# A two-layer graph network on one core: projecting with the sums as the stationary operand, 14 node slots per tile, and a new table of tiles looked up by TensorE

## The reference, cut to what matters

```python
h = relu(layernorm(x))
# layer 0: a row of 9 edge coefficients times the source's 32 features, contracted with W
x = x + segment_sum(einsum over (coef9[e], h[src[e]], W), dst)
h = relu(layernorm(x))
# layer 1: 16 basis coefficients by relation, times an attention scalar, and the last edge's self loop
a   = tanh(relu(sum(x_hat * y_hat) / sqrt(32)))      # x_hat from h[src], y_hat from h[dst], relation
msg = einsum("eb,ebo->eo", w_comp[etype], einsum("ei,bio->ebo", h[src], weight))
x = x + relu(segment_sum(a * msg, dst) + h[src[last edge]] @ self_loop_weight)
```

## Time and profile before

| what | value |
| --- | --- |
| median of the runs | 3294.89 us |
| time of the profiled execution | 3295.84 us |
| its span in the trace | 3294.0 us |
| PE busy | 2972.4 us, 90% |
| PEld busy | 2392.0 us, 73% |
| DVE busy | 2602.5 us, 79% |
| POOL busy | 2414.9 us, 73% |
| ACT busy | 895.1 us, 27% |
| POOL's gathers, L541 | 2541, mean 946 ns |
| found rows, L609 | 8190 matmuls, mean 372 ns |

### The profile page before, as it was taken

The page is one execution under the profiler, slowest core; times in us unless marked ns, Lnnn a source line. Parts: engine busy times, 40 slices in busy tenths (PEclk is TensorE's granted clock), DMA queues, the critical chain, the costliest instruction groups (busy, mean ns, idle before and its releaser), DMA issues.

```text
span 3294.0 us, 108331 instructions
## 1 busy us (share of the span) xinstructions
PE 2972.4 (90%) x41934; PEld 2392.0 (73%) x41934; DVE 2602.5 (79%) x3897; ACT 895.1 (27%) x1910; POOL 2414.9 (73%) x2546
## 2 busy tenths in 40 slices
PE   2999999999999999999789999999999999899997
PEld 2777777777777777777677777777777777777776
DVE  7777777777777777777678888888888888888886
ACT  1111111111111111111344444444444444444342
POOL 6777777777777777777377777777777777777774
PEclk9999999999999999999789999999999999999998
DMA  4111111111111111111233333333333333332331
GB/s 138 28 28 28 28 28 28 27 28 27 28 27 29 27 29 27 29 27 29 67 55 58 55 59 59 57 56 59 58 57 56 59 58 58 55 58 54 58 57 40
DMA packets 220288, 150.94 MB, mean 46 GB/s; under 512 B 122954, under 2 KB 201083, under 8 KB 219901
## 3 DMA queue, kind: packets, MB, share of 16 engines
q0 software_dynamic: 81312, 41.79, 12.3%
q1 hardware_dynamic: 138013, 100.79, 12.3%
q10 hardware_dynamic: 576, 2.40, 0.2%
HBM read 136.54 MB, written 8.22 MB: 44 GB/s over the span
## 4 chain that ended last, share of the span: by engine, by line
PE 32%; POOL 9%; issue 5%; DVE 4%; DVEq 1%; DMA 0%; ACT 0%; POOLq 0%; ACTq 0%
PE ps L609 17%; POOL xg L541 9%; PE ps L634 5%; PE ps L675 4%; PE ps L622 3%; DVE scratch L960 2%; PE ps L657 1%; PE ps L572 1%; PE ps L645 1%; DVE Z L1044 0%; DMA xg<-h_table,idx 0%; DVE aggT L1062 0%; DVEq L960 0%; DVE blocks L951 0%; DVEq L1062 0%
## 5 line engine op out<-in xcount | busy, mean ns | idle before, releaser
L541 POOL DMA_INDIRECT xg<-h_table,idx x2541 | 2404.1, 946 | 844.1 <-issue 758.9
L609 PE MATMUL ps<-h,blocks 128*128 128x448 f32 x8190 | 1803.0, 372 | 237.5 <-DVE scratch L960 213.4
L609 PEld LDWEIGHTS ps<-h,blocks 128*128 128x128 f32 x8190 | 1501.3, 188 | 458.5 <-issue 324.1
L1044 DVE TENSOR_TENSOR Z<-coef,ps 128x864 f32<-128x864 f32 (+1 forms) x522 | 734.4, 1448 | 16.6 <-DVE ps L985 0.2
L951 DVE TENSOR_TENSOR blocks<-scratch,ps 128x896 fp32r<-128x896 int16 x585 | 630.1, 1077 | 34.4 <-PE ps L609 34.4
L675 PE MATMUL ps<-Z,xg 128*32 128x32 f32 (+3 forms) x25008 | 507.8, 215 | 8.3 <-DVE Z L1044 7.9
L675 PEld LDWEIGHTS ps<-Z,xg 128*32 128x32 f32 x25008 | 403.9, 110 | 93.0 <-issue 70.2
L1062 DVE TENSOR_TENSOR aggT<-aggT,ps 64x128 f32 (+1 forms) x262 | 74.1, 283 | 485.1 <-PE ps L657 478.4
L960 DVE SCALAR_TENSOR_TENSOR scratch<-ramp_sb,scratch,ps 128x448 f32<-128x448 f32 x585 | 396.7, 678 | 7.8
L830 ACT ACTIVATE p_left<-ps 96x128 f32<-96x128 f32 (+2 forms) x262 | 64.6, 246 | 1189.3 <-PE ps L645 1140.8
L965 DVE TENSOR_REDUCE xg<-scratch 128x32 f32<-128x448 f32 x585 | 362.8, 620 | 20.2
(11 more groups left out here) (105 smaller groups left out, 1109.4 us busy)
## 6 DMA issues: line engine op xcount, KB each, us to landing
xg<-h_table,idx POOLq DMA_INDIRECT x2541
rows_b<-typ_short SPq DMA_DIRECT2D x130, 258.0 KB
scratch<-q_short SPq DMA_DIRECT2D x260, 96.0 KB
rows_b<-dst_short SPq DMA_DIRECT2D x130, 126.0 KB
coef<-in_edge_dram SPq DMA_DIRECT2D x130, 54.0 KB
att_tab<-p_table SPq DMA_DIRECT2D x393, 8.1 KB
p_table<-Z SPq DMA_DIRECT2D x8, 297.0 KB, 3.9
X<-in_x_dram SPq DMA_DIRECT2D x7, 224.0 KB, 4.6
```

The lines of the kernel that those rows point to most:

```text
L541: pool.indirect_dma_start(xg[:, g.q, t - g.s * J, :], None, h_table[n], bass.IndirectOffsetOnAxis(ap=idx[:, t:t + 1], axis=0)).then_inc(L. ...
L609: last = pe.matmul(found_ps[b], blocks[:, b, c, :], h_2[:, a, c], start=(c == 0 and a == 0), stop=(c == NCH - 1 and a == 1))
L1044: dve.tensor_tensor(Z[:, b, js, 0:C * WN].rearrange("p j (c n) -> p j c n", n=WN), coef[:, js, :].unsqueeze(3).broadcast_to([P, k, C, WN]) ...
```

## The change

- WN is 14 in place of 16. HW, the width of a half group, becomes 84 in place of 96. `Z` and the startup tables share a buffer `room` of fixed size.
- `project` has the sums stationary (84 columns) and the weights moving (64 or 32 columns), one chain over c for each half: 6 matmuls in place of 3 in layer 0, 10 in place of 5 in layer 1. Its result has nodes on partitions. `copy_oT`, `turn` and their buffers are gone.
- `place_rows` of g-2 comes after tile 4 of the 12 in `sum_edges`, where `turn` was, in place of after tile 8.
- `copy_o` comes ahead of the attention in ScalarE's step.
- `NP` has an entry for each group. Layer 0: 2 in the first 8 and last 8 groups, else 3, 3, 3, 2 in turn, 346 found tiles in place of 325. Layer 1: 3 in every fourth group from 8 to 116, else 2, 288 in place of 260.
- ScalarE, VectorE and SyncE have 16 steps straight, 11 rounds of a loop of eight steps, and the rest straight. The flag `beyond` is read at step 16 on each engine, in place of after the steps.
- TensorE waits for the last `added` itself; VectorE's wait and signal for it are gone.

```diff
-WN = 16
+WN = 14
 JH = J // 2
 HW = JH * WN
 NCH = 7
 MC = M // NCH
-NP = [[3, 2, 3, 2], [2, 2, 2, 2]]
+EIGHT = 8
+LOOP = [2, FULL // EIGHT - 3]
+NP = [[2 if s < 8 or s >= FULL - 8 else [3, 3, 3, 2][s % 4] for s in range(FULL)], [3 if 8 <= s < FULL - 10 and s % 4 == 0 else 2 for s in range(FULL)]]
 NPM = max(max(np) for np in NP)
...
-    return len(range(q, FULL, 4)) * (J - NP[n][q]) + (JT if q == FULL % 4 else 0)
+    return sum(J - np for np in NP[n][q::4]) + (JT if q == FULL % 4 else 0)
+
+
+def in_loop(count, i, r):
+
+    if isinstance(i, int):
+        return count(i * EIGHT + r)
+    at = LOOP[0] * EIGHT + r
+    return count(at) + (i - LOOP[0]) * (count(at + EIGHT) - count(at))
 
 
...
             return gathers_of_pass(n, self.q)
-        return (self.i + self.r // 4 + 1) * (J - NP[n][self.q])
...
 
-        return self.nj if self.tail else J - NP[n][self.q]
+        return self.nj if self.tail else J - NP[n][self.of_loop()]
...
         if self.tail:
             return []
-        np = NP[n][self.q]
-        return [(NPM - np + i, J - np + i, (sum(NP[n][0:self.q]) + i) % 2, self.tiles_before(n) + i + 1) for i in range(np)]
+        at = self.of_loop()
+        np = NP[n][at]
+        return [(NPM - np + i, J - np + i, (sum(NP[n][0:at]) + i) % 2, self.tiles_before(n) + i + 1) for i in range(np)]
 
 
...
-def over_steps(eng, k, body, lag):
+def over_steps(eng, k, body, lag, look):
 
 
     def step(i, r):
-        body([Group(i, r - d, k) if not isinstance(i, int) or 0 <= i * 4 + r - d < NG else None for d in range(lag + 1)])
-    for t in range(4):
+
+        body([Group(i, r - d, k) if not isinstance(i, int) or 0 <= i * EIGHT + r - d < NG else None for d in range(lag + 1)])
+    for t in range(LOOP[0] * EIGHT):
         step(0, t)
-    with eng.Fori(0, FULL // 4 - 1) as i:
-        for u in range(4):
-            step(i, 4 + u)
-    for t in range(FULL // 4 * 4, NG + lag):
+    too_far = look(eng) if isinstance(k, int) else None
+    with eng.Fori(*LOOP) as i:
+        for u in range(EIGHT):
+            step(i, u)
+    for t in range(LOOP[1] * EIGHT, NG + lag):
         step(0, t)
-
-
-def all_steps(body, lag):
+    return too_far
+
+
+def all_steps(eng, body, lag, look):
 
     for s in range(NG + lag):
+        if s == LOOP[0] * EIGHT:
+            too_far = look(eng)
         body([Group(0, s - d, 0) if 0 <= s - d < NG else None for d in range(lag + 1)])
+    return too_far
 
...
-        oT_ps = ps[0:2 * F, 4, :]
-        o_ps = ps[0:HW, 4, 2 * HW:2 * HW + 4 * F].rearrange("p (h o) -> p h o", h=2)
-        win_ps = ps[0:3 * F, 4, 2 * HW + 4 * F:2 * HW + 4 * F + P]
+        o_ps = ps[0:HW, 4, 0:4 * F].rearrange("p (h o) -> p h o", h=2)
+        win_ps = ps[0:3 * F, 4, 4 * F:4 * F + P]
...
-        Z = sb("Z", [P, 2, J, C1 * WN])
-
-
-        room = Z[:].rearrange("p b j z -> p (b j z)").bitcast(I32)
+        room = sb("room", [P, max(2 * J * C1 * WN, 4 * T)], I32)
+        Z = room[:].bitcast(F32)[:, 0:2 * J * C1 * WN].rearrange("p (b j z) -> p b j z", b=2, j=J)
         dst_all, dnext_all, first_all, group_all = (room[:, i * T:(i + 1) * T] for i in range(4))
...
+        def look_beyond(eng):
+
+            eng.wait_ge(beyond_set, 1)
+            return eng.value_load(beyond[0:1, 0:1], min_val=0, max_val=1)
+
         def all_passes(eng, passes, restart=None, finish=None):
 
-            passes(0)
-            eng.wait_ge(beyond_set, 1)
-            too_far = eng.value_load(beyond[0:1, 0:1], min_val=0, max_val=1)
+            too_far = passes(0)
             with eng.If(too_far):
                 if restart:
...
                     for s in range(NG):
+                        if s == LOOP[0] * EIGHT and isinstance(k, int):
+                            too_far = look_beyond(pool)
                         gather(Group(0, s, k))
+                    return too_far
 
                 all_passes(pool, one_pass)
...
                     pe.wait_ge(L.G_set, g.order())
-                    wait(pe, L.oT_set, g.order() - 1)
+                    wait(pe, L.o_set, g.order() - 1)
                     wait(pe, L.added, g.order() - 1)
-                    for c in range(cq):
-                        rows = P if c < cq - 1 else F
-                        last = pe.matmul(oT_ps[0:no, 0:hh * w], weights[0:rows, c, :], G_sb[0:rows, c, 0:hh, 0:w],
-                                         start=(c == 0), stop=(c == cq - 1))
+                    for h in range(hh):
+                        for c in range(cq):
+                            rows = P if c < cq - 1 else F
+                            last = pe.matmul(o_ps[0:w, h, 0:no], G_sb[0:rows, c, h, 0:w], weights[0:rows, c, :],
+                                             start=(c == 0), stop=(c == cq - 1))
                     last.then_inc(L.projected, 1)
-
-                def turn(g):
-                    hh, w = g.halves()
-
-                    pe.wait_ge(L.oT_set, g.order())
-                    wait(pe, L.o_set, g.order() - 1)
-                    pe.nop().then_inc(L.turn_go, 1)
-                    for h in range(hh):
-                        last = pe.transpose(o_ps[0:w, h, 0:no], oT_sb[0:no, h, 0:w], ident[0:no, 0:no])
-                    last.then_inc(L.turned, 1)
 
                 def place_rows(g):
...
@@ -678,8 +685,6 @@
                         if j == g.nj - 1:
                             last.then_inc(L.summed, 1)
                         if back and j == min(g.nj, J // 3) - 1:
-                            turn(back)
-                        if back and j == min(g.nj, 2 * J // 3) - 1:
                             place_rows(back)
 
                 def step(gs):
@@ -693,18 +698,16 @@
                     if gs[1]:
                         sum_edges(gs[1], gs[2])
                     elif gs[2]:
-                        turn(gs[2])
                         place_rows(gs[2])
 
...
             edge_sums(0)
-            pe.wait_ge(sums_done, 1)
+            pe.wait_ge(layers[0].added, NG)
...
 
-                def copy_oT(g):
+                def copy_o(g):
                     hh, w = g.halves()
                     act.wait_ge(L.projected, g.order())
-                    wait(act, L.turned, g.order() - 1)
-                    act.activation(oT_sb[0:no, 0:hh, 0:w], oT_ps[0:no, 0:hh * w].rearrange("p (h w) -> p h w", h=hh),
-                                   ACT.Copy).then_inc(L.oT_set, 1)
-
-                def copy_o(g):
-                    hh, w = g.halves()
-                    act.wait_ge(L.turned, g.order())
                     wait(act, L.placed, g.order() - 1)
                     act.activation(o_sb[0:w, 0:hh, 0:no], o_ps[0:w, 0:hh, 0:no], ACT.Copy).then_inc(L.o_set, 1)
...
                         one_hots(gs[0])
+                    if gs[2]:
+                        copy_o(gs[2])
                     if n == 1 and gs[1]:
                         attention(gs[1])
-                    if gs[2]:
-                        copy_oT(gs[2])
-                        copy_o(gs[2])
 
...
                 all_passes(dve, one_pass, restart, lambda: dve.wait_ge(L.added, (PASSES + 1) * NG))
-
-                dve.wait_ge(L.added, NG)
-                dve.nop().then_inc(sums_done, 1)
```

More of the change, by code:

```diff
@@ L86 @@
 assert NOWHERE < 1 << 15 and NREL <= 1 << 8
-assert NCH * MC == M and FULL % 2 == 0 and all(sum(np) % 2 == 0 for np in NP) and JT <= JH and PS <= P
+assert NCH * MC == M and FULL % 2 == 0 and all(sum(np) % 2 == 0 and len(np) == FULL for np in NP) and JT <= JH and PS <= P
 def gathers_of_pass(n, q):
-    return len(range(q, FULL, 4)) * (J - NP[n][q]) + (JT if q == FULL % 4 else 0)
+    return sum(J - np for np in NP[n][q::4]) + (JT if q == FULL % 4 else 0)
[4 more added lines that the diff above has]
+    return count(at) + (i - LOOP[0]) * (count(at + EIGHT) - count(at))
 class Group:
@@ L122, in full_order2 @@
     def full_order2(self):
-        return self.k * len(range(self.b, FULL, 2)) + self.i * 2 + self.r // 2 + 1
+        return self.k * len(range(self.b, FULL, 2)) + in_loop(lambda s: s // 2 + 1, self.i, self.r)
     def gathers(self, n):
@@ L129, in gathers, with of_loop @@
             return gathers_of_pass(n, self.q)
-        return (self.i + self.r // 4 + 1) * (J - NP[n][self.q])
+        return in_loop(lambda s: sum(J - np for np in NP[n][s % 4:s + 1:4]), self.i, self.r)
+    def of_loop(self):
+        return self.s if isinstance(self.s, int) else LOOP[0] * EIGHT + self.r
     def gathered_tiles(self, n):
-        return self.nj if self.tail else J - NP[n][self.q]
+        return self.nj if self.tail else J - NP[n][self.of_loop()]
     def tiles_before(self, n, later=0):
-        r = self.r + later
-        of_pass = FULL // 4 * sum(NP[n]) + sum(NP[n][0:FULL % 4])
-        return self.k * of_pass + (self.i + r // 4) * sum(NP[n]) + sum(NP[n][0:r % 4])
+        return self.k * sum(NP[n]) + in_loop(lambda s: sum(NP[n][0:max(s, 0)]), self.i, self.r + later)
     def found_tiles(self, n):
@@ L845, in one_pass @@
```

(2 more changed lines are left out.)

31 lines of the change are left out of this document (13 added, 18 removed).

## The result

The changed kernel takes 3237.36 us (median of 4 runs, 3235.66 to 3238.09) against 3295.61 us before in the same series (3294.35 to 3296.37): ratio 0.9823, 95% interval 0.9809 to 0.9837. The forecast was 3282. The direction and the range hold, the size doesn't: 58 us are gained where 13 were forecast.

What follows compares the result with a forecast made beforehand. TensorE's path, with VectorE's chain in it, was taken to bound layer 0 and two thirds of layer 1, gathers the rest. Layer 0 -25, layer 1 +16, ends -4 gave -13 us: 3282 us for the median, range 3222 to 3330.

Steps and rivals of the forecast that it cites:

- Who sets the groups: Both layers: TensorE's path, including VectorE's place, add and pick, sets layer 0 and two thirds of layer 1; gathers the rest.
- Projection: TensorE, each group: 1.42 us in layer 0, 0.17 more than before; 1.88 us in layer 1, 0.03 more.
- Rival C: Projection on TensorE: each record pays load and stream, 0.43 us more than forecast each; 3394 us, slower; chance 0.08.
- Turn and placing: From the sums' start to `place`, turn gone and four tiles fewer: 0.82 us saved in layer 0, 0.91 in layer 1.
- Groups of layer 0: Layer 0: 131 x (0.17 - 0.82) = -85 us, plus 21 x 2.88 = +60 us: -25 us.
- 14 slots: VectorE in layer 1: `Z`, 2 x 1.85 us, gets 0.44 us shorter.
- The attention behind the copy: Layer 1: attention 1.06 us later, `add` reached 0.62 later against 0.94 slack; two-tile groups gain 0.32 us, not 0.88.
- Found tiles: A third found tile adds 2.88 us to TensorE's path; GpSimd loses 21 and 28 gathers, 26 and 35 us.
- Ends: Each layer's end: turn, copy and the flag's load go, 2 us a layer, -4 us in all.
- rival B: Gathers bind, if attention costs no path time or projection is shorter: 3231 us, down to 3206; chance 0.25.
- Rival D: VectorE's path is longer than reckoned; layer 1's two-tile groups take 12.2 us, 30 us more: 3312 us; chance 0.17.
- E: The general passes run; the widest tile spans 11 nodes, under 14, so no chance worth a number.

Runs made afterwards that it cites:

- the control: The changed kernel run again without an edit, beside the kernel before, in two series: 3236.32 us (ratio 0.9818) and 3235.61 us (ratio 0.9820).

## Why the prediction was wrong in size

- **Who sets the groups: right.** Layer 0 and three-tile groups go by the loop of placing, add, pick and find; two-tile groups of layer 1 by VectorE behind the tanh. The experiment with the old order shows the latter.
- **Projection: right.** 1.39 and 1.89 us against 1.42 and 1.88; the load sets the distance (96 against 84 columns), with 75 ns a record where 70 was forecast. Rival C falls with it: it gave 1.85 us in layer 0. The Trainium skill (TensorE: Matmul & The Clock Gate, Part 3: Packing small matmuls) lets weight loads overlap running matmuls only where the row group differs, which is what C worked out. The records of one chain use the same rows, and at 75 ns a record in place of C's 123 the trace disagrees with the rule. One reading in the forecast is wrong without effect: the distance formula that it quotes from the Trainium skill gives 12 x 29 + 370 ns = 0.72 us and 20 x 16 + 370 = 0.69, and not its lower bound of 1.0 and 0.91.
- **The entry: the missing term.** The accounting charged drains for 32 rows and at the projection's end, but had none at its start, where the old one went from 128 stationary columns to 64 or 32. It goes for good: 0.08 us a group in layer 0 and 0.10 in layer 1 on the mean, 259 x 0.09 = 23 us if all of it reached the end; its shares are in the items below.
- **Turn and placing: right.** From the sums' start to the placing 0.81 us less in layer 0 (0.82 forecast) and 0.92 in layer 1 (0.91).
- **Groups of layer 0: too small a gain.** The forecast had 0.65 us a group; a two-tile group gained 0.79 and a three-tile one 0.72. The entry gives 0.08 more and the projection 0.04, since it costs 0.13 and not 0.17; from the placing to the add it is 0.02 longer; and in two-tile groups the way from the add to the next find is 0.05 shorter, for which I have no cause. By the count of groups, 44 x 0.14 + 86 x 0.07 = 12 us, of which 11 to 15 show.
- **14 slots: right in layer 1.** `Z` lost 3.62 - 3.19 = 0.43 us (0.44 forecast).
- **The attention behind the copy: the step that failed.** With this term the forecast had layer 1 become 16 us longer, and it is 21 us shorter. I had the coefficients 1.06 us later. They come 5.52 us after the find in place of 4.76, 0.76 later. Of the 0.3 that was too much, 0.11 is the entry, and 0.13 a wait that isn't there: I let the relu start when the copy ends, plus a gap (0.25 us behind its start), and it starts 0.12 behind it, while the copy still runs (2220.68 and 2220.80 above). The forecast's own sum with 0.76 is 0.94 - (0.76 - 0.44) = 0.62 a group in place of 0.32, and 12.19 - 0.62 = 11.57 where 11.61 was measured. The two kinds of groups give 101 x 0.29 + 28 x 0.2 = 35 us, against the 37 that layer 1 misses.
- **Found tiles: right.** A third one costs 2.83 (2.88). The lead of layer 0 held, but barely: at its end 5.8 us of it are left, and 4.7 are left where the gathers bind. That the range of the lead was enough was assumed and not worked out, and so in part luck.
- **Ends: 0, not -4.** They are below what I can tell apart.

In the profiled executions the miss is 15 us in layer 0, 37 in layer 1 and -5 at the ends, 47 in all; the medians give 45. The time fell near rival B's 3231, but not by its mechanism: no group waited for gathers (23.4 us ahead at the end of layer 1), and the attention did cost time. It took one more edit to get there; the order put back is what rival B describes, and the gathers then bind from about group 62 on, with layer 1 at 1549.9 us, where the 1584 before less B's 35 are 1549. Rival D had the right place and the wrong sign, and E never came up.

## What to carry to other kernels

When a step is moved between two others, price the gaps on both sides of it from a row, not only the step: an entry gap of 0.09 us, 260 times, was as large as the projection's own change. An order on a third engine is worth reading against the slack of the engine that waits for it: 0.12 us of copy ahead of two short instructions cost 0.5 us a group, since that copy itself waits for TensorE. And two resources that are near to each other must be moved together: with TensorE's loop shortened by about 0.3 us a group the gathers took 29 of 39 us back, so the split of tiles between them is the next thing to set.

## What the runs showed of the hardware

A change from 128 stationary columns to 64 costs TensorE about 0.09 us (float32), one to 66 or 84 none (3.00 and 2.91 us from find to projection); the records behind the change lose another 0.05 us (1.26 and 1.21 us from the projection to the next find). ScalarE started an instruction 0.12 us after the start of a 0.22 us copy on which it doesn't depend (2220.68 and 2220.80). Float32 records with 84 and 96 stationary columns and 64 streamed stand 75 and 85 ns apart. And on two chips TensorE ran 8.7 to 9.9 matmul records a us on the mean of the windows above, where the control has 12.8 and 15.4, at a granted clock of 0.80 to 0.91 and not 1.00: the kernel before took 4925 to 5015 us there and 3294 to 3296 elsewhere, at the same code.
